# A fused attention and expert kernel on one core: the opening reordered, and idle matmuls put into it

## The reference

```python
# layer 1: queries come from x, keys and values from x and from the context (77 rows a batch)
q = layer_norm(x) @ Wq;  k, v = split(concat(layer_norm(context), layer_norm(x)) @ Wkv)
q, k = l2norm(q) * q_scale, l2norm(k) * k_scale            # 8 heads of 64
x = x + layer_norm(softmax(mask(8 * q @ k.T)) @ v @ Wo)
x = x + quantized_matmul(layer_norm(x), weight_q) * weight_scale + bias     # layer 2
x = x + softmax(layer_norm(x) @ We @ context.T) @ context @ W2.T            # layer 3, softmax over queries
x = x + expert[argmax(t @ Wr.T + br)](t),  t = layer_norm(x)                # layer 4, 8 experts of 128-512-128
```

## Time and profile before

| | us |
|---|---|
| median of 3 runs (955.83 to 957.16) | 955.97 |
| the profiled execution | 956.35 |
| its span, first to last instruction | 954.6 |
| PE busy in it (95% of the span) | 906.6 |
| DVE / ACT / POOL busy | 745.8 / 693.6 / 459.0 |

### The profile page before, as it was taken

How to read it: one execution, slowest core, us unless ns; L and a number is a source line. 1 busy time by engine, 2 the same in 40 slices (tenths; PEclk the granted TensorE clock), 3 DMA queues, 4 the chain that set the end, 5 groups by cost and what they waited for, 6 DMA issues and landing times.

```text
span 954.6 us, 30726 instructions
## 1 busy us (share of the span) xinstructions
PE 906.6 (95%) x11238; PEld 788.0 (83%) x11238; DVE 745.8 (78%) x2524; ACT 693.6 (73%) x1671; POOL 459.0 (48%) x1094
## 2 busy tenths in 40 slices
...
DMA packets 45193, 31.44 MB, mean 33 GB/s; under 512 B 11555, under 2 KB 40166, under 8 KB 45046
## 3 DMA queue, kind: packets, MB, share of 16 engines
...
## 4 chain that ended last, share of the span: by engine, by line
PE 68%; DVE 15%; ACT 8%; POOL 4%; issue 4%; DMA 0%; DVEq 0%; POOLq 0%; SPq 0%; ACTq 0%
PE ps L1652 9%; PE ps L1605 9%; PE ps L1580 7%; PE ps L1698 6%; PE ps L1396 5%; PE ps L1567 5%; PE ps L1559 5%; PE ps L1398 5%; PE ps L1397 5%; DVE sumsq L1292 4%; PE ps L1657 3%; PE ps L1682 2%; ACT probs L593 2%; ACT qk_hat L606 2%; PE ps L1435 1%
## 5 line engine op out<-in xcount | busy, mean ns | idle before, releaser
L1324 DVE TENSOR_TENSOR qk_hat<-ps,rstd 128x512 f32<-128x512 f32 x168 | 106.4, 685 | 50.1 <-POOL rstd L835 50.1
L1292 DVE TENSOR_REDUCE sumsq<-qk_hat 128x8 f32<-128x512 f32 x168 | 107.8, 678 | 34.6 <-ACT qk_hat L606 33.5
L828 POOL TENSOR_TENSOR rs_t<-rs_y 128x32 f32<-128x32 f32 x73 | 17.5, 240 | 234.7 <-ACT rs_y L647 234.7
L1605 PE MATMUL ps<-v_x,prob 128*64 128x65 f32 x2048 | 127.9, 225 | 2.1 <-ACT w_all L617 0.4
L1605 PE MATMUL ps<-v_c,prob 128*64 128x65 f32 x2048 | 124.3, 222 | 0.0
L1396 PE MATMUL ps<-w_hi,xc_hi 128*128 128x512 f32 x272 | 121.6, 447 | 2.3 <-POOL xc_lo L802 2.3
L666 ACT ACTIVATE prob<-ps,neg_shift 128x512 f32<-128x512 f32 x128 | 88.4, 691 | 48.6 <-PE ps L1652 48.6
L606 ACT ACTIVATE qk_hat<-ps 128x512 f32<-128x512 f32 x168 | 98.7, 599 | 33.5 <-PE ps L1398 27.9
L1605 PEld LDWEIGHTS ps<-v_x,prob 128*64 128x64 f32 x2048 | 105.0, 137 | 20.9 <-issue 19.3
L1652 PE MATMUL ps<-qT_all,kT_all 64*128 64x128 f32 x1536 | 111.6, 285 | 2.9 <-ACT w_all L617 1.2
L1398 PE MATMUL ps<-w_hi,xc_lo 128*128 128x512 f32 x272 | 108.0, 397 | 0.0
...
...
...
## 6 DMA issues: line engine op xcount, KB each, us to landing
...
out_dram<-prob,x_res POOLq DMA_INDIRECT x71, 2.3
sorted_rows<-stage,idx POOLq DMA_INDIRECT x64, 2.4
...
```

What stands on the lines that cost most here:

```text
L1292: nc.vector.reduce_sum(sumsq[:, n * H:(n + 1) * H], sq[:, n * INNER:(n + 1) * INNER].rearrange("p (h d) -> p h d", d=DH), AX).then_inc(ss_ ...
L1324: nc.vector.tensor_tensor(qk_hat[:, n * INNER:(n + 1) * INNER].rearrange("p (h d) -> p h d", d=DH), ps_qk[:, n, :].rearrange("p (h d) -> p ...
L1605: last = nc.tensor.matmul(dst[half:half + DH, :], prob[:, kt, col + half:col + half + DH], v, start=kt == 0, stop=kt == 1)
```

## The change

- Transfers: on SP's queue the second lot of tokens is asked for straight behind the norm columns, ahead of the experts; experts 1 and 2 wait for that lot; `ask(2)` and expert 4 come ahead of the second layer's weights. On ACT's queue Wq and Wkv come behind the table load and two small column transfers; the first 4 mask pieces follow, the other 8 are issued after round -3 on ACT, and Wo after round -2.
- DVE: the statistics of the first tokens wait on the transfer's own semaphore; the cast that makes `w_hi` also waits for `var_ready`; `w_lo` is made behind the first `xc_hat`, in three parts; the third batch's statistics and the sums of squares of batch 0 come ahead of batch 1's `xc_hat`.
- PE: 32 transposes of the identity into bank 0 ahead of round -2, and 16 behind it; they compute nothing that is read. Experts 0 and 1 are transposed ahead of batch 1's tokens.
- Copies of the experts' weights: DVE takes numbers 2 and 3 of the six instead of 0 and 1; ACT's four are spread through round -1, and its second copy of round 0 comes behind the first exponential.
- The second layer's weights are cast, transposed and copied in rounds 4 and 5 instead of -1 and 0; ACT's query copy no longer waits for the mask's bias, and PE waits for it only ahead of the second value product of round 0. POOL's zeroing of lot 2's context blocks and its constants move into round -1.

```diff
-            sp.wait_ge(mask_zeroed, 1)
-            for to, src in itertools.islice(mask_pieces(), ON_SP):
-                sp.dma_start(to, src).then_inc(ld_w, 16)
-            arrived(0)
             ask(1)
             sp.dma_start(qs_b[:, :], q_scale.partition_broadcast(P)).then_inc(ld_w, 16)
             sp.dma_start(ks_b[:, :], k_scale.partition_broadcast(P)).then_inc(ld_w, 16)
-            for e in range(AHEAD):
-                expert(e)
+            arrived(0)
+            expert(0)
             arrived(1)
+            expert(1)
+            expert(2)
             sp.dma_start(lno_w[:, :], ln_o_w.partition_broadcast(P)).then_inc(ld_late, 16)
             sp.dma_start(lno_b[:, :], ln_o_b.partition_broadcast(P)).then_inc(ld_late, 16)
+            expert(3)
+            ask(2)
+            expert(4)
+            arrived(2)
             for to, src in ((wq_raw[:, :], weight_q), (we_raw, We), (w2_raw, W2),
...
-            expert(AHEAD)
-            ask(2)
-            for e in range(AHEAD + 1, E):
+            for e in range(5, E):
                 expert(e)
-            arrived(2)
...
-            act.dma_start(w_raw[:, 0:INNER], Wq).then_inc(ld_qkv, 16)
-            act.dma_start(w_raw[:, INNER:3 * INNER], Wkv).then_inc(ld_qkv, 16)
             nc.scalar.preload_act_table_set("natural_log_exp_and_others")
 
...
-            act.dma_start(wo_sb[:, :, :], Wo.rearrange("(t p) d -> p t d", p=P)).then_inc(ld_late, 16)
...
+            scale_columns(0, q_scale)
+            act.dma_start(w_raw[:, 0:INNER], Wq).then_inc(ld_qkv, 16)
+            act.dma_start(w_raw[:, INNER:3 * INNER], Wkv).then_inc(ld_qkv, 16)
+            scale_columns(1, k_scale)
             act.wait_ge(mask_zeroed, 1)
-            for to, src in itertools.islice(mask_pieces(), ON_SP, None):
-                act.dma_start(to, src).then_inc(ld_w, 16)
+            masks(0, FIRST_MASKS)
...
-                    act.wait_ge(setup_v, SETUP_V)
+                    act.wait_ge(setup_v, SHIFT_V)
...
-                    act.wait_ge(s["wT_done"], 2 * (j + AHEAD) + 2)
-                    nc.scalar.activation(w2_all[:, j + AHEAD, 0:F], ps[:, 3, :], ACT.Copy).then_inc(s["w_copied"], 1)
+                    if j > 0:
+                        second_weights(j)
...
+                if not inside and j == -1:
+                    first_weights((0,))
                 roots()
...
                 if not inside and j == -1:
-                    first_weights()
+                    first_weights((1,))
...
+                if not inside and j == 0:
+                    second_weights(j)
...
+                if not inside and j == -1:
+                    first_weights((4, 5))
 
             act.wait_ge(setup_g, FIRST_G)
             run(-3, 1, 3, -3, False, -3, 0)
+            masks(FIRST_MASKS, None)
             act.wait_ge(ld_ln, 4 * 16)
             run(-2, 0, 0, -2, False, -2, 0)
+            act.dma_start(wo_sb[:, :, :], Wo.rearrange("(t p) d -> p t d", p=P)).then_inc(ld_late, 16)
...
+                    if not inside and j == -1:
+                        nc.gpsimd.memset(ctx_res[:, packed[2], :], 0.0).then_inc(ctx_zeroed, 1)
...
+                if not inside and j == -1:
+                    second_setup()
...
+            def high_weights():
 
                 dve.wait_ge(ld_qkv, 32)
+                dve.wait_ge(var_ready, 1)
                 nc.vector.tensor_copy(w_hi[:, :], w_raw[:, :]).then_inc(setup_v, 1)
+
+            def low_weights():
+
                 dve.wait_ge(setup_v, 2)
-                nc.vector.tensor_tensor(w_lo[:, :], w_raw[:, :], w_hi[:, :].bitcast(F32), ALU.subtract).then_inc(setup_v, 1)
+                for n in range(3):
+                    part = slice(n * INNER, (n + 1) * INNER)
+                    last = nc.vector.tensor_tensor(w_lo[:, part], w_raw[:, part], w_hi[:, part].bitcast(F32), ALU.subtract)
+                last.then_inc(setup_v, 1)
...
+            def sums_of_squares(j, pos):
+
+                for n in range(3) if fresh(pos + 1) else range(2):
+                    dve.wait_ge(sq_done, 3 * j + 4 + n)
+                    nc.vector.reduce_sum(sumsq[:, n * H:(n + 1) * H],
+                                         sq[:, n * INNER:(n + 1) * INNER].rearrange("p (h d) -> p h d", d=DH),
+                                         AX).then_inc(ss_raw, 1 if n == 0 or fresh(pos + 1) else 2)
+                dve.wait_ge(ss_raw, 3 * j + 6)
+                if j == -1:
+                    dve.wait_ge(rs_ready, 2)
+                nc.vector.tensor_scalar(var_in[:, 0:3 * H], sumsq[:, :], L2_EPS * L2_EPS, None,
+                                        ALU.max).then_inc(ss_done, 1)
+
+            def third_tokens():
+
+                dve.wait_ge(tokens_in, 3)
+                nc.vector.bn_stats(bn6[:, 0, :], one(x_res, 2)).then_inc(xc_bn, 1)
+                dve.wait_ge(xc_bn, 3)
+                nc.vector.bn_aggr(xc_stat[:, 0, 0, :], bn6[:, 0, :]).then_inc(xc_mv, 1)
...
+                if has(j + 3, inside) and (inside or j != -1):
+                    if not inside and j == -3:
+                        dve.wait_ge(ld_lot[0], 16 * (1 + len(list(context_pieces(packed[0])))))
+                    else:
+                        dve.wait_ge(tokens_in, j + 4)
...
                 if not inside and j == -3:
-                    split_weights()
+                    high_weights()
                 if not inside and j == -2:
                     scales()
+                    third_tokens()
+                    sums_of_squares(-1, -1)
                 if not inside and j == -1:
                     first_weights()
...
+                if not inside and j == -3:
+                    low_weights()
...
-                    dve.wait_ge(ld_late, N_LATE)
                     bias_of_mask()
                     setup_second()
+                    dve.wait_ge(ld_late, N_LATE)
+                if not inside and j == SECOND_J - 1:
+                    dve.wait_ge(second_in, 16 * SECOND)
+                    nc.vector.tensor_copy(wq_f, wq_raw[:, :]).then_inc(s["setup_d"], 1)
...
+            def first_weights(some):
+
+                for n, bank, w in first_flips():
+                    if n in some:
+                        pe.wait_ge(ld_exp[n // 2], 32)
+                        if n > 3:
+                            pe.wait_ge(s["w_copied"], n - 3)
+                        flip(bank, w).then_inc(s["wT_done"], 1)
+
             def slot_a(j, rho, g, inside):
 
-                if not inside and j == 0:
+                if not inside and j == SECOND_J:
 
                     pe.wait_ge(s["setup_d"], 1)
-                    pe.wait_ge(s["w_copied"], 4)
-                    pe.wait_ge(setup_v, SETUP_V)
...
-                    if j == 0:
-                        pe.wait_ge(s["setup_c"], 3)
+                    if j < 2:
+                        pe.wait_ge(s["w_copied"], 4 + 2 * j)
...
-                if not inside and 0 <= j < E - AHEAD:
+                if not inside and 0 < j < E - AHEAD:
                     pe.wait_ge(s["w_copied"], 4 + 2 * j + 2)
+                if not inside and j == SECOND_J:
+                    pe.wait_ge(s["setup_c"], 3)
...
+                        if not inside and j == 0 and kt == 1:
+                            pe.wait_ge(setup_v, SETUP_V)
...
+                if not inside and j == -1:
+                    first_weights((0, 1, 2, 3))
...
+            def keep_busy(n):
+
+                for i in range(n):
+                    nc.tensor.transpose(ps[:, 0, 0:P], ident[:, :], ident[:, :])
+
             pe.wait_ge(setup_g, FIRST_G)
             run(-3, 1, 3, -3, False, -3, 0)
+            keep_busy(32)
             run(-2, 0, 0, -2, False, -2, 0)
+            keep_busy(16)
             pe.wait_ge(setup_g, SETUP_G)
             pe.wait_ge(setup_v, 3)
...
-                    for n, bank, w in first_flips():
-                        pe.wait_ge(ld_exp[n // 2], 32)
-                        if n > 3:
-                            pe.wait_ge(s["w_taken"], n - 3)
-                        flip(bank, w).then_inc(s["wT_done"], 1)
-                    pe.wait_ge(s["w_copied"], 1)
+                    first_weights((4, 5))
+                    pe.wait_ge(s["w_taken"], 1)
```

83 lines of the change are left out of this document (40 added, 43 removed).

## The result

The changed kernel takes 953.98 us in the median of 17 runs (951.17 to 955.27), the kernel before 955.96 (955.46 to 957.38): a ratio of 0.9976, with a 95% interval of 0.9969 to 0.9983. It is faster by 2.0 us, where 4.75 were forecast. The profiled execution of the changed kernel is the second shortest of its 17: 952.38 us, against 956.35 for the profiled one of before. So 4.0 of the forecast 4.75 us stand in its trace, and the rest of this text is mostly about why other executions have less. The spread is itself a result: 4.1 us over 17 runs (1.9 before), and the longer executions have the lower mean granted clock (0.999 at 951.17, 0.997 at 952.38 to 953.88, 0.994 to 0.995 at 954.76 to 955.27).

The account below looks back on a forecast made before the run. The prediction took PE to bound the rounds, so an earlier round 1 reaches the end nearly whole. Terms 2.4 + 0 + 1.2 + 1.35 + 0.15 - 0.35 = 4.75 us gave 951.6 profiled, median 951.2, range 949.3 to 954.0.

Parts of the forecast that it names:

- first `rstd`: Opening up to the first `rstd`: earlier tokens and POOL freed from `w_lo` and the cast; gain 2.4, from 1.2 to 3.1.
- `rstd` to first product: Opening, from first `rstd` to PE's first product: steps unchanged, `w_lo` parts hardly in the way; gain 0, bounds -0.9 and +0.2.
- first product to third `rstd`: Batch 0's products at PE's high rate save 1.7, less 0.6 for late masks; gain 1.2, bounds 0 and 1.8.
- third `rstd` to first value product: Before round 1: PE's wait for and transposes of the second layer's weights go; gain 1.35, bounds 0.9 and 1.6.
- to round 2: Later in round 0: PE's wait of 1.23 for ACT's copy goes; gain 0.15, up to 0.5.
- to 710 to 715 us: Round 5: the second layer's three transposes come back inside PE's dense time; loss 0.35.
- behind, to the end: Rest of the kernel: no term of its own, the opening's gain reaching the end nearly whole; 0.
- The clock does not hold: Rival: PE stays at or falls back to 1.2 GHz before the products; gain 2.75, time 953.2; chance 0.14.
- The other transfers I cost at nothing: Opening: experts 1 and 2 and lot 2 cost 0; a microsecond's lateness would not delay `qk_hat` until used up.
- Transfers take back part: Rival: Wkv, masks or experts 1 and 2 land 1 to 3 us late; 953.2, from 952.5 to 955; chance 0.14.
- Slower: Rival: early transposes spend the clock's rise, it falls ahead of the product until after round 0; 959; chance 0.06.
- The change is hidden: Rival: POOL stays blocked by DVE in new places, the rounds swallow the rest; gain under 1.9, 955.5; chance 0.08.

Follow-up runs that it names:

- e15: The changed kernel, unedited, run once more for a third profile; one execution, 954.85 us.
- e1: The changed kernel without the 48 useless transposes on PE; 952.03 us, ratio 0.9958 to the kernel before.
- e6: The changed kernel without the useless transposes and with expert 1 asked for ahead of the second lot; ratio 0.9948 to the kernel before.
- e8: The changed kernel with expert 1 early and the weights' split undone (`w_lo` one instruction straight after the cast); ratio 0.9954 to the kernel before.
- e10: The changed kernel with two broadcast scale transfers ahead of the second lot on SP's queue, delaying that lot; 956.07 us, ratio 0.9994 to the kernel before.
- e13: e10 with ACT's eight mask transfers moved behind round -2's ACT work; one execution, 961.37 us, the mask late by design.
- e11: The changed kernel with the second lot asked for first and expert 1 ahead of SP's wait for it; 950.40 us, ratio 0.9933 to the kernel before.
- e7: The kernel before with only the 48 useless transposes added; ratio 0.9991 to the kernel before.
- e5: The changed kernel run again unedited, in a batch where everything ran about 20 us slower; ratio 0.9957 to the kernel before.
- e3: The changed kernel with expert 1's two transfers issued ahead of SP's wait for the second lot; 951.14 us, ratio 0.995 to the kernel before.
- e9: The changed kernel with the second lot asked for at 2.2 us instead of 4.5, small column transfers swapping queues; 950.72 us, ratio 0.9937 to the kernel before.
- e2: The changed kernel with 20 more useless transposes filling PE's waits; 951.51 us, ratio 0.9957 to the kernel before.

## Why the prediction was wrong, point by point

The sum, term by term, with e15 as the execution near the long end and the first profile near the short one (each difference is taken between the same rows as in the forecast):

| term | forecast | first profile | e15 |
|---|---|---|---|
| first `rstd` | 2.4 | 3.04 | 3.14 |
| `rstd` to first product | 0 | 0.11 | 0.13 |
| first product to third `rstd` | 1.2 | 1.43 | -0.04 |
| third `rstd` to first value product | 1.35 | 0.02 | -1.01 |
| to round 2 | 0.15 | 0.01 | -0.14 |
| to 710 to 715 us | -0.35 | -0.28 | -0.29 |
| behind, to the end | 0 | -0.36 | -0.29 |
| sum | 4.75 | 3.97 | 1.50 |

The median, 953.98, lies inside the stated range, at its edge of 954.0; the range had room for it because a cold clock and late transfers were taken in, not because the terms came true.

**First `rstd`: the mechanism right, the size short.** The tokens landed at 3.9, outside the bounds of 5.0 to 6.2; that this is for want of weights ahead of them is argued, not tested. ACT's 0.85 us behind its own mask issues was not in the forecast at all; I had moved the masks past SP's work but not past ACT's. That the issues hold ACT is seen across the runs: in e1 to e6, e8, e10, e13 and e15 `rs_ln` starts at 6.21 to 6.23 although `var_in` ends anywhere from 5.38 to 6.06, and in e11, where the four issues end at 5.68, it starts at 5.78. So the tokens' early landing was not used in full: in e6 their statistics start at 4.67 instead of 3.97, and the first `rstd` is ready at 8.87, no later than the 8.96 of the first profile. The cast's cost to POOL was 0.95 - 0.26 = 0.7 us, not the 0.35 counted. In e8 the same cast and `w_lo` stretch two other Newton instructions to 0.86 and 0.65 us, for 0.25 each. The rule quoted from the Trainium skill, "SBUF — State Buffer", "SBUF: two separate sides", would have said 0.93 for the cast; the 0.7 us of the trace lie nearer to it than to my figure.

**To the first product: right.** 3.66 us for 3.77. POOL's `xc_hi` took 0.60 instead of 0.40 beside a part of `w_lo`, the 0.2 that stood as the bound. The 32 transposes did raise the rate, and it held over the gaps to the product in each profile of the changed kernel. Beside e7 one sees how near that was: there a gap of 4.08 us let it fall, and the 16 transposes cost 0.6 us ahead of the product, the first half of the rival *The clock does not hold*.

**First product to third `rstd`: right in the first profile, gone in e5 and e15.** The masks cost DVE 0.64 us of waiting, as forecast. What failed is the sentence that the second lot "lands at about 11.2 and is not in the way": its statistics start at 12.17, 13.37 and 13.57 us in the three profiles of this kernel, asked for 1.9 us earlier than before (4.46 for 6.36) and used at about the same time (13.17 before). On DVE seven scale instructions, the third tokens and the three sums stand behind it, and on ACT the squares that the sums need: in e5 and e15 the third `rstd` follows it by 6.92 us, and the products' gain is gone.

**Third `rstd` to round 1: the step that failed** (forecast a gain of 1.35, measured 0.02, -0.53 in e5 and -1.01 in e15), and with it "The other transfers I cost at nothing", above all "not `qk_hat`, until that microsecond is used up". e3 and e9 show the term when nothing is in its way: 22.48 - 20.09 = 2.39 and 20.79 - 18.40 = 2.39 us from the third `rstd` to the value product, a gain of 4.16 - 2.39 = 1.77, even over the upper bound of 1.6. In the changed kernel two things take it away. One is the late transfer. The forecast has expert 2 land 1 us behind expert 1, at 17.5, with 4.7 us from the issue of its second half; in the first profile SP issues that half at 13.57 and PE, waiting for it, starts at 19.41, 5.8 us later, and in e5 and e15 it is 6.3 us. From the start of expert 2's transposes to the value product it takes 2.27 us at the high rate (e1: 20.98 to 23.25; e2: 20.20 to 22.47), so they have to start by 0.12 us behind the third `rstd` (2.39 - 2.27). They start 0.27, 0.76 and 0.78 behind it in the first profile, e5 and e15, late by 0.15, 0.64 and 0.66. The other, larger one is the clock: the same stretch takes 3.87, 3.93 and 4.39 us, 1.60, 1.66 and 2.12 more. The sums, 1.75, 2.30 and 2.78, are the whole of what lies over 2.39 (4.14, 4.69, 5.17).

So the forecast assumed that the rate holds, argued from gaps of 1.22 and 1.23 us, and looked for the danger ahead of the product. The danger was behind it: between 15.8 and 20.9 us PE has only 19 transposes to do, of weights, tokens and mask, and it waits for expert 1, for `xc_hat` and for expert 2. e5 and e1 are the cleanest pair: expert 2's transposes start at 21.05 and 20.98, but the value product comes at 24.98 with the fall and at 23.25 without. The rows of e5, to be set beside those of e1 above:

```profile
21.05 1.65 PE L1463 MATMUL ps<-ident,w_all 128*128 128x128 f32 x8 [1.87 <-DMA w_all<-in_L_ffn_W_dram]
24.98 0.48 PE L1450 MATMUL ps<-w_hi,xc_hi 128*128 128x512 f32 x1
```

The Trainium skill's rule from "TensorE: Matmul & The Clock Gate", Part 1, quoted in the forecast, that idleness restores half rate, agrees with the falls at 20.0, 21.4 and 19.3 us, each of which followed waits of PE; I had applied it to one gap only.

**What came true of the rivals.** *Transfers take back part* named the place, with 953.2, but as a loss in itself, and it got 0.14 where it deserved more: the transfer's own lateness is the smaller half, and its price comes through the clock. *Slower* had half of the mechanism, an early rise that is spent in waits; it placed the fall ahead of the first product, where it came behind the products and was over before round 1, at a smaller size. *The change is hidden* did not happen: rounds 2 and later pass on what the opening gives. The 0.3 us that goes behind 715 us was not followed up.

**Left open.** Why SP takes 1.87 to 3.43 us to issue five transfers of the second lot, and 5.11 and 4.69 when it starts at 6.1 (but 1.98 in the kernel before, where it starts at 6.80), was not found; e13 only excludes the mask transfers beside it. The wait of ACT for its mask issues was not removed by a kernel of its own; in e11 `rstd` is ready at 7.83 and `xc_hat` starts at 8.69, right behind the cast, so there at least Wkv's landing and not ACT is the limit. That part was not tried further.
